# A four-layer graph network in one pass: the low half of the messages moves from VectorE to Pool

## The reference, cut to what matters

```python
def _ggc(x, adj, W, wih, whh, bih, bhh):
    m = adj @ (x @ W)
    gi = m @ wih.T + bih
    gh = x @ whh.T + bhh
    ...
    r = jax.nn.sigmoid(i_r + h_r)
    z = jax.nn.sigmoid(i_z + h_z)
    n = jnp.tanh(i_n + r * h_n)
    return (1.0 - z) * n + z * x
h = jax.nn.relu(_ggc(x, adj, W1, ...))
return jax.nn.relu(_ggc(h, adj, W2, ...))
```

## Time and profile before

| what | value |
|---|---|
| time, median of 3 runs | 458.71 us (458.45 to 458.75) |
| time of the profiled execution | 457.77 us |
| its span | 456.0 us |
| mean granted clock of PE | 0.985 |
| PE busy | 428.1 us, 94% |
| DVE busy | 283.2 us, 62% |
| ACT busy | 197.8 us, 43% |
| POOL busy | 114.9 us, 25% |

### The profile page before, as it was taken

The page is one execution under the profiler, slowest core; times in us unless marked ns, Lnnn a source line. Parts: engine busy times, 40 slices in busy tenths (PEclk is TensorE's granted clock), DMA queues, the critical chain, the costliest instruction groups (busy, mean ns, idle before and its releaser), DMA issues.

```text
span 456.0 us, 6313 instructions
## 1 busy us (share of the span) xinstructions
PE 428.1 (94%) x2294; PEld 214.0 (47%) x2294; DVE 283.2 (62%) x777; ACT 197.8 (43%) x335; POOL 114.9 (25%) x155
## 2 busy tenths in 40 slices
PE   5399799999999999999999999999999999999992
PEld 1134244444344444455555545554545655465571
DVE  3575969666964896463667526868742566175453
ACT  2277567766876687506555414445111121100000
POOL 8111614210510020014122111343330444211011
PEclk9889999999999999999999999999999999999997
DMA  8999999999999991000011010000000111101000
GB/s 117 155 163 108 107 107 107 109 113 110 107 110 112 109 99 25 0 7 18 13 24 24 13 23 1 2 1 0 2 0 1 23 24 24 24 12 36 12 13 23
DMA packets 24895, 23.70 MB, mean 52 GB/s; under 512 B 14369, under 2 KB 16289, under 8 KB 24865
## 3 DMA queue, kind: packets, MB, share of 16 engines
q0 software_dynamic: 9360, 16.78, 36.7%
q1 hardware_dynamic: 15216, 6.33, 5.8%
q10 hardware_dynamic: 288, 0.20, 0.2%
HBM read 69.44 MB, written 1.05 MB: 155 GB/s over the span
## 4 chain that ended last, share of the span: by engine, by line
PE 85%; DVE 6%; DMA 3%; ACT 2%; issue 2%; POOL 1%; POOLq 0%; DVEq 0%; ACTq 0%
PE Y L887 46%; PE both L800 17%; PE Y L779 8%; PE Y L791 3%; PE both L760 2%; PE both L763 2%; DMA xrow<-in_xrow 2%; DVE work L550 2%; PE both L755 2%; PE both L766 1%; PE both L807 1%; PE both L768 1%; DMA adjT<-in_adjT 1%; ACT wgt L353 1%; DVE work L555 1%
## 5 line engine op out<-in xcount | busy, mean ns | idle before, releaser
L887 PE MATMUL Y<-adjT,S 128*128 128x512 fp8e4 (+1 forms) x1056 | 232.7, 373 | 1.0 <-POOL S L252 0.7
L887 PEld LDWEIGHTS Y<-adjT,S 128*128 128x128 f16 x1056 | 102.8, 99 | 110.2 <-POOL S L252 1.2
L353 ACT ACTIVATE wgt<-both 128x512 int16<-128x512 f32 x192 | 113.9, 597 | 44.3 <-PE both L800 36.8
L237 POOL TENSOR_TENSOR rstd<-stat,mhalf 128x4 f32<-128x4 f32 (+2 forms) x29 | 34.0, 1173 | 195.0 <-DVE stat L457 195.0
L800 PE MATMUL both<-adjT,fix 128*128 128x512 fp8e4 x192 | 73.8, 384 | 1.0 <-ACT wgt L353 0.5
L800 PE MATMUL both<-adjT,tri 128*128 128x512 fp8e4 x192 | 74.2, 387 | 0.0
L779 PE MATMUL Y<-wgt,S 128*128 128x512 bf16 x192 | 73.8, 384 | 0.0
L265 POOL DMA_DIRECT2D adjT<-in_adjT x63 | 33.7, 570 | 68.3 <-DMA adjT<-in_adjT 68.3
L550 DVE SCALAR_TENSOR_TENSOR work<-work,adjT 128x1024 int16<-128x1024 int16 x32 | 42.7, 1356 | 0.0
L555 DVE SCALAR_TENSOR_TENSOR work<-adjT,work 128x1024 int16<-128x1024 fp8e4 x24 | 29.4, 1225 | 16.7 <-ACT work L350 15.0
L800 PEld LDWEIGHTS both<-adjT,fix 128*128 128x128 bf16 x192 | 18.9, 98 | 38.8 <-ACT wgt L353 17.8
(11 more groups left out here) (112 smaller groups left out, 422.1 us busy)
## 6 DMA issues: line engine op xcount, KB each, us to landing
adjT<-in_adjT POOLq DMA_DIRECT2D x63, 256.0 KB, 39.0
out_rows<-xrow SPq DMA_DIRECT2D x7, 128.0 KB, 1.9
xrow<-in_xrow SPq DMA_DIRECT2D x1, 640.0 KB, 8.7
hrow<-in_w_gates SPq DMA_DIRECT2D x1, 512.0 KB, 13.5
biases<-in_biases SPq DMA_DIRECT2D x1, 416.0 KB, 7.7
x<-S SPq DMA_TRANSPOSE x24, 2.4
xrow<-in_xrow SPq DMA_DIRECT2D x1, 256.0 KB, 4.1
adjT<-in_adjT POOLq DMA_DIRECT2D x2, 128.0 KB, 6.3
```

The lines of the kernel that those rows point to most:

```text
L237: nc.gpsimd.tensor_tensor(rstd[:, 0:blocks], stat[:, 2, 0:blocks], mhalf[:, 0:blocks], ALU.pow)\
L353: nc.scalar.activation(wgt[:, c, tiles % 2, :], V[c][:, :], ACT.Relu).then_inc(w_ready[c], 1)
L887: mm = nc.tensor.matmul(bank(layer, g)[:, 0:nb * P], S[layer % 2][:, jb, :], cols[:, jb, :], start=(jb == 0), stop=(jb == JB - 1), skip_gr ...
```

## The change

`m_lo` is taken out of DVE's program and put into Pool's. Its instruction is the same, now issued to Pool, with waits for what stands before it on Pool. In layer 1, Pool runs `m_lo` of group g + 1 ahead of `split_rows(1, g)`; in layer 2, ahead of `root` of group g. The first message of each layer is done before the loop. On DVE, `take_y` gets a wait for the message that used the same buffer before.

```diff
             def split_rows(layer, g):
 
                 blk = slice(g * B, (g + 1) * B)
+                if layer == 1:
+                    pool.wait_ge(m_ready, min(g + 2, G))
                 pool.wait_ge(rows_ready, (layer - 1) * G + g + 1)
...
+            def m_lo(e):
+
+                pool.wait_ge(m_hi, e - G + 1)
+                if e == G:
+                    pool.wait_ge(dinv_pow, 1)
+                elif e == 2 * G:
+                    pool.wait_ge(s_ready, 3 * G)
+                elif e not in (G + 1, 2 * G + 1):
+                    pool.wait_ge(s_ready, e + G - 1)
+                nc.gpsimd.tensor_tensor(m16[0:D, e % 2, :], m[D:P, e % 2, :], m16[D:P, e % 2, :], ALU.subtract)\
+                    .then_inc(m_ready, 1)
+
+            m_lo(G)
             for g in range(G):
+                if g < G - 1:
+                    m_lo(G + g + 1)
                 split_rows(1, g)
             pool.wait_ge(dinv_ready, 2)
+            m_lo(2 * G)
             for layer in (2, 3, 4):
                 for g, (_, nb) in enumerate(UNITS[layer]):
                     n = Q + (layer - 2) * G + g
+                    if layer == 2 and g < G - 1:
+                        m_lo(2 * G + g + 1)
+                        pool.wait_ge(m_ready, G + g + 2)
                     root(n, nb)
...
-            def m_lo(e):
-
-                dve.wait_ge(m_hi, e - G + 1)
-                nc.vector.tensor_tensor(m16[0:D, e % 2, :], m[D:P, e % 2, :], m16[D:P, e % 2, :], ALU.subtract)\
-                    .then_inc(m_ready, 1)
...
                 if g == 0:
                     take_y(layer, 0)
-                    m_lo(e)
                 if g < G - 1:
+                    if e >= G + 1:
+                        dve.wait_ge(m_ready, e - G)
                     take_y(layer, g + 1)
...
-                if g < G - 1:
-                    m_lo(e + 1)
                 dve.wait_ge(n_ready, e - G + 1)
```

## The result

| | before | after |
|---|---|---|
| time, median of 4 runs | 458.73 us (458.45 to 458.75) | 463.63 us (463.37 to 463.99) |
| span of the profiled execution | 456.0 us | 461.8 us |
| mean granted clock of PE | 0.985 | 0.987 |
| PE busy | 428.1 us | 429.2 us |
| DVE busy | 283.2 us | 273.7 us |

The kernel is slower: ratio 1.0109, 95% interval 1.0091 to 1.0126, or 4.90 us between the medians. DVE lost 9.5 us of busy time and Pool gained 20.2 us, which answers to the earlier trace rows. The work of PE is the same; it waits more. Of the 5.8 us between the two spans, 1.1 us lies ahead of the first combine of layer 1.

The account below looks back on a forecast made before the run. PE was taken to set the pace, so a lighter DVE gains nothing. Losses of 4.2 + 0.2 + 0.6 = 5.0 us on the 458.71 us median gave 463.7 us, range 460.2 to 465.8.

Parts of the forecast that it names:

- The part removed: Sixteen DVE instructions of 0.69 us, 11.0 us of DVE work, go at zero gain, beside a PE that never stops.
- The ring: Layer 1: combine through split rows and Pool's message to the next combine takes 7.12 us against 6.07 between matmuls.
- signs named: PE waits on Pool's line five times in layer 1, four about 1.0 us, one 0.2; about 0.9 at layer 2's head.
- The duration on Pool: The message instruction on Pool takes 1.28 us, with a lower bound of 0.61 and an upper of 1.61.
- The sum: Layer 1's four steps 4.2 us, combine 6 0.2, layer 2's head 0.6, rest of layer 2 0; total 5.0 us.
- Contention: DVE operations with two SBUF inputs stand still while Pool works; costed at 0 in layer 1, within slack in layer 2.
- the slack: Rest of layer 2: next combine possible at C + 7.12, PE wants it at 7.80 us, leaving 0.68 us of cover.
- The delayed norm in layer 2: Layer 2: Pool's message meets DVE's norm, which loses time; covered by slack, so no cost.
- The short instruction: Rival: Pool's message takes 0.61 us, layer 1 loses 1.5 us, time 460.2 us; chance 0.12.
- The longer ring: Rival: message 1.61 us, or 1.28 with Pool held behind DVE; ring 7.45 us, time 465.7 us; chance 0.16.
- No gain: Rival: lighter DVE shortens PE's two waits, at most 1.1 us, time 457.6 us; chance 0.03.
- fall of the clock: Rival: PE's clock falls in the new pauses, which are 1 in 7; chance 0.02, inside the high side.

Follow-up runs that it names:

- swap_and_ahead: Kernel before with all messages on Pool, layer 1's ahead of the rows' subtraction, and ACT's high part of the rows ahead of the seed: ratio 0.9992.
- ring_on_vector: Kernel before, messages on DVE, one added wait holding layer 1's groups 2 to 7 until Pool finished the rows split two groups before: ratio 1.0038.
- swap_after: Kernel after the change, with ACT doing the high part of the rows ahead of the seed; Pool's order stays: ratio 1.0009.
- ahead_of_low_rows: Kernel after the change, with layer 1's message on Pool moved between the scaling and the subtraction of the split rows: ratio 1.0005.
- only_layer1: Kernel after the change, with only layer 1's eight messages on Pool and layer 2's back on DVE: ratio 1.0091.
- half_and_half: Kernel after the change, with columns 0 to 255 of each message on Pool, the rest on DVE at its old place: ratio 1.0064.
- half_one_count: As half_and_half, but both halves count on one semaphore, so PE's combine has a single wait for the message: ratio 1.0057.

## Why the prediction was right, point by point

Forecast 463.7 us, measured 463.63. The mechanism, the places and the sizes hold, but an agreement to 0.1 us is in part chance: the duration was given too long, and a handover in the ring and a start at the head that came later than forecast made up for about half of that in the ring and most of it at the head. The steps of it:

- **The part removed brings nothing.** Right: no step got shorter than before, and swap_and_ahead, where nothing else stands in its way, is 0.59 us slower in the trace than the same swap with the messages on DVE.
- **The ring.** Right, in place and in kind. Its length was given as 7.12 us and is 7.05. Link by link: 5.61 forecast, 5.62 measured; from Pool instruction to Pool instruction 0.08, measured 0.14; the message 1.28, measured 1.15; to PE 0.15, measured 0.14. The link 0.08 was read from another pair of instructions. So 0.13 us too much and 0.06 too little leave 0.07 a step. Of the signs named, six waits on Pool's line, five of them in layer 1, the one of 0.2 us at combine 6 isn't in the list, though its step is 0.13 us longer and Pool's message ends 0.14 us before it (253.91 + 1.16, combine 6 at 255.21): too short a loss to show. The four others are listed with 0.82 and not 1.0 us.
- **The duration on Pool.** 0.13 us too long, well between its bounds. What was mis-sized is the fixed part: 54 ns was taken from the float32 lines, but for this subtraction the two lengths on 64 partitions give 2 x 0.668 - 1.152 = 0.184 us, and doubling L252 less that gives the measured 1.15. The lower bound, time by the total of elements, is refuted: 64x256 takes 0.668 us, as 128x256 does (0.667 at least), and half the partitions buy nothing. By the Trainium skill, GPSIMD Engine Reference, 3.1, the estimate was 1.12 us; the measured 1.15 lies nearer to it than to mine. That, too, is in part chance: this subtraction has the larger fixed part, but costs less an element than the float32 lines, (1152 - 668) / 256 = 1.89 ns against 2.18.
- **The sum.** Four steps 4 x 1.05 = 4.2, measured 28.20 - 24.27 = 3.9; combine 6 0.2, measured 7.06 - 6.93 = 0.13; head 0.6, measured 0.56 (the instruction 0.13 us shorter than forecast, its start 0.10 later: 277.49 - 262.57 against 272.24 - 257.42); rest of layer 2 at 0, measured 0.12. Together 4.75 us against the 5.0 of the forecast; the medians differ by 4.9.
- **Contention.** Costed at 0 in layer 1, which holds. Its rule, that DVE operations with two SBUF inputs stand still, was read too narrowly from its own rows: L687, which took 0.83 us beside L252, has only one, and its pair takes 0.36 us in ring_on_vector, where Pool stands idle beside it. In layer 2 it was put in the slack, and there the step before layer 3 has none: L254 takes 0.87 us against 0.73, since DVE, 0.3 us earlier than before, had just begun L706. The row of POOL and then that of DVE after:

```profile
323.93 0.87 POOL L254 TENSOR_TENSOR S<-work,S 128x256 f16<-128x256 f32 x1 [2.52 <-ACT S L355]
```

```profile
323.79 0.48 DVE L706 SCALAR_TENSOR_TENSOR work<-work,xrow 128x128 f32<-128x128 f32 x2
```

  This is the one term that was missed: 0.12 us. The lighter DVE is the likely cause, for L672 to L692 come 0.3 us earlier with it; no run moved DVE alone.
- **The delayed norm in layer 2.** Right: one pair of it takes 1.44 us instead of 0.48 beside the message, and no step of layer 2 but the one named and the head is longer. It didn't fall on L672, which was named as a sign: its pair takes 0.49 us as before and comes 0.3 us earlier, and the waiting is in the norm behind. With it DVE's busy time fell by 9.5 us where about 11 were forecast. Timeline of DVE after, iteration 2:

```profile
300.82 1.44 DVE L476 TENSOR_TENSOR work<-work 128x128 f32<-128x128 f32 x2
302.19 0.47 DVE L477 TENSOR_REDUCE stat<-work 128x2 f32<-128x128 f32 x2
```

- **The rivals.** The short instruction falls with 1.15 us. The longer ring isn't there after the change, but swap_after shows its mechanism at 0.14 us a step. No gain and no fall of the clock were seen.

## What to carry to other kernels

Before work is moved to an engine that looks idle, write down what stands ahead of it in that engine's order and what that waits for: here a message whose input was ready 3 us early stood behind rows whose high part came only late in the iteration, and so the idle engine set the pace of the busy one. Compare the length of the ring that this closes with the work between two turns of it; the share of busy time says nothing on it. A move can be kept if the place is right (ahead_of_low_rows gives back all of layer 1), but it only gains where the relieved engine stood on the path, and here a swap of two instructions on a third engine was worth more than the whole move.

## What the runs showed of the hardware that was not expected

- **Which of Pool and DVE waits can go either way at the same distance, and is worth 0.4 us.** Before the change, L252 starts at 318.22 and DVE's pair of two-input operations 0.13 us later. Timeline of DVE before:

```profile
317.94 0.49 DVE L674 TENSOR_TENSOR work<-work 128x128 f32<-128x128 f32 x2
318.35 0.96 DVE L692 SCALAR_TENSOR_TENSOR work<-work,xrow 128x128 f32<-128x128 f32 x2
```

  Pool takes 0.73 us and DVE's pair 0.96, so DVE waits. In only_layer1 the same two stand 0.13 us apart as well, 323.96 and 324.09 (shown above), and now DVE's pair takes its 0.49 us while Pool takes 1.14, 0.47 over its shortest: about the length of the pair, which fits a Pool that waits. PE waits for this subtraction, and the step is 8.68 instead of 8.28 us. ring_on_vector shows the same 1.14 and 8.68. Within a trace the outcome doesn't change: in each of the five iterations 1 to 5 of layer 2, Pool takes 0.73 or 0.74 us before the change, and 1.14 in only_layer1 and ring_on_vector. What tips it wasn't tried; with one trace of each kernel, it isn't shown that it is the kernel and not the execution. The Trainium skill, SBUF — State Buffer, section SBUF: two separate sides, has the lock go to the one that starts first; on these rows the start times don't tell which that is. DVE's L674 (L694 in only_layer1), the pair ahead, began 0.28 us before Pool in both kernels, with opposite outcomes.
- **Pool's time for this subtraction goes by the length in a partition and not by the partitions**: 64x256 in 0.668 us, 64x512 in 1.15, 128x256 in 0.667. By the first two it has a fixed part of about 0.18 us; by the float32 lines of the earlier trace rows only 0.05.
- **A second wait on PE** ahead of the matmul that was being waited for cost 0.11 us (half_and_half against half_one_count), though what it waited for was already done.
